# Cross-attention keys turned by VectorE in 32x32 blocks, scores on eight 32x64 tiles of TensorE, and each step's keys in two parts

## The reference

```python
scores = jnp.einsum('bsh,bqh->bsq', encoder_outputs, hidden)     # hidden = layernorm(x)
attn_weights = jax.nn.softmax(scores, axis=1)                    # over the keys s
context = jnp.einsum('bsq,bsh->bqh', attn_weights, encoder_outputs)
x = x + context
```

## Time and profile before

| | |
|---|---|
| median of three runs | 1027.85 us |
| profiled execution, span from first to last instruction | 1027.4 us |
| PE busy | 926.9 us, 90% |
| DVE busy | 484.5 us, 47% |
| ACT busy | 327.8 us, 32% |
| cross-attention, to the start of the next sublayer's projections (L544) | 320 us |
| one of its steps, from scores to scores | 37.4 us |

### The profile page before, as it was taken

How to read it: one execution, slowest core, us unless ns; L and a number is a source line. 1 busy time by engine, 2 the same in 40 slices (tenths; PEclk the granted TensorE clock), 3 DMA queues, 4 the chain that set the end, 5 groups by cost and what they waited for, 6 DMA issues and landing times.

```text
span 1027.4 us, 14956 instructions
## 1 busy us (share of the span) xinstructions
PE 926.9 (90%) x5233; PEld 678.6 (66%) x5249; DVE 484.5 (47%) x1124; ACT 327.8 (32%) x860; POOL 342.7 (33%) x170
## 2 busy tenths in 40 slices
PE   5999999999989997799897999979998999998960
PEld 5645645655646866788775667657876888886840
DVE  5723523433445025444467676786355333333404
ACT  3303412421433212655215565652330221111210
POOL 0000000000033233436101523454376999991015
PEclk9999999999999798899999999989999999998985
DMA  9642651561442003001109000003048344451117
GB/s 347 263 188 76 250 226 67 218 255 68 188 174 82 1 1 124 1 1 38 31 13 377 1 1 0 1 1 123 2 153 292 106 158 165 169 184 41 51 50 225
DMA packets 41257, 121.00 MB, mean 118 GB/s; under 512 B 3696, under 2 KB 7792, under 8 KB 37120
## 3 DMA queue, kind: packets, MB, share of 16 engines
q1 hardware_dynamic: 32320, 100.52, 26.0%
q10 hardware_dynamic: 6336, 11.54, 3.3%
q0 software_dynamic: 2560, 8.39, 2.5%
HBM read 102.05 MB, written 18.38 MB: 117 GB/s over the span
## 4 chain that ended last, share of the span: by engine, by line
PE 75%; POOL 7%; DVE 5%; DMA 5%; issue 4%; ACT 3%; SPq 0%; POOLq 0%; ACTq 0%; DVEq 0%
PE bank L499 9%; PE bank L457 8%; PE bank L477 7%; PE bank L955 5%; PE bank L957 5%; PE bank L956 5%; PE bank L771 2%; DMA nat<-in_ctx_keys 2%; PE bank L728 2%; PE bank L657 2%; PE bank L544 2%; POOL x_slots L1163 2%; PE bank L784 2%; PE bank L546 1%; PE bank L545 1%
## 5 line engine op out<-in xcount | busy, mean ns | idle before, releaser
L1193 ACT COPY ctxT<-bank 128x512 f32<-128x512 f32 (+1 forms) x104 | 60.1, 578 | 188.5 <-PE bank L457 187.7
L457 PE MATMUL bank<-cst,nat 128*128 128x128 f32 (+1 forms) x832 | 101.9, 278 | 10.4 <-DMA nat<-in_ctx_keys 9.8
L1049 POOL TENSOR_TENSOR wq_lo<-wq_raw,wq_hi 128x1024 fp32r<-128x1024 f32 x4 | 9.3, 2360 | 296.8 <-ACT wq_hi L1241 296.8
L457 PEld LDWEIGHTS bank<-cst,nat 128*128 128x128 f32 (+1 forms) x832 | 89.3, 143 | 22.3 <-issue 8.3
L499 PE MATMUL bank<-nat,probT 128*64 128x512 f32 (+1 forms) x416 | 91.0, 594 | 3.9 <-ACT probT L1199 3.9
L477 PE MATMUL bank<-ctxT,qT 128*64 128x400 f32 (+1 forms) x512 | 87.5, 499 | 0.8 <-DVE qT L1549 0.8
L1193 DVE COPY ctxT<-bank 128x512 f32<-128x512 f32 (+1 forms) x104 | 69.8, 671 | 31.1 <-PE bank L457 30.3
L1177 POOL TENSOR_TENSOR ring_lo<-ring_raw,ring_hi 128x2048 fp32r<-128x2048 f32 x18 | 82.9, 4604 | 1.4
L1103 POOL TENSOR_TENSOR sp<-sp,s_inv 128x512 f32<-128x512 f32 x32 | 32.6, 1040 | 139.9 <-DVE s_inv L1861 139.9
L955 PE MATMUL bank<-ring_hi,xg_lo 128*128 x176 | 73.4, 417 | 0.4 <-DVE y L2074 0.4
L477 PEld LDWEIGHTS bank<-ctxT,qT 128*64 128x64 f32 x512 | 37.2, 136 | 50.8 <-issue 49.8
(11 more groups left out here) (273 smaller groups left out, 2054.4 us busy)
## 6 DMA issues: line engine op xcount, KB each, us to landing
nat<-in_ctx_keys SPq DMA_DIRECT2D x32, 1536.0 KB, 12.7
ring_raw<-in_Wexp SPq DMA_DIRECT2D x21, 1024.0 KB, 9.2
x_slots<-zeros SPq DMA_DIRECT2D x1, 5632.0 KB, 25.7
hn<-x_slots ACTq DMA_DIRECT2D x22, 256.0 KB, 3.0
y_slots<-hn ACTq DMA_DIRECT2D x22, 256.0 KB, 2.1
w_raw<-in_Wexp SPq DMA_DIRECT2D x3, 1024.0 KB, 10.0
nat<-in_ctx_keys SPq DMA_DIRECT2D x16, 130.0 KB
wq_raw<-in_Wq SPq DMA_DIRECT2D x1, 2048.0 KB, 8.0
```

What stands on the lines that cost most here:

```text
L457: last = nc.tensor.transpose(bank[4 + g % RING][:, c * P:c * P + n], nat[par][0:n, b, j, c * P:(c + 1) * P], ident[0:n, 0:n])
L1193: copy(ctxT[b][:, :, j * P:j * P + n], src).then_inc(sem_done, 1)
```

## The change

Seven edits that belong together.

1. TensorE's key transposes, their ring of banks and the copies out of them go. VectorE turns the keys itself with its 32x32 block transpose, straight from `nat` to `ctxT` (`columns`): every 32x32 block is turned in place, so feature block j (of 16) of the keys in partition strip i (of 4) lies in strip i. `ctxT` is now [128, 2, 16, 416]: feature within the block in the partition, 13 x 32 keys a strip.
2. The scores contract over 32 features at a time. A matmul takes strip i, batch b and feature block j: 32 rows by 64 columns of the array, and the keys of strip i go to PSUM bank i (`scores4`, one tensor over banks 0 to 3). Sixteen feature blocks accumulate. A step has 2 parts x 16 x 2 x 4 = 256 such matmuls where it had 32.
3. The queries must stand in the same 32-row strips, four times: query_transposes is 64 matmuls with 32 output columns against the identity, into banks 4 to 7, copied to `q4` (in `hn`'s space) by ScalarE (three) and VectorE (one).
4. A step's keys are turned and scored in two parts, blocks 0 to 6 and 7 to 12 (`PARTS`); VectorE's four pairs of transposes for the next step are put between its other work.
5. The keys are loaded in three pieces as the context product releases them (`PIECES`, `context_part`), and the first step's in four (`FIRST`).
6. Because the probabilities stand in the order of the blocks, the exponentials read `scores4` across banks: three of 512 elements, one of 64, one of 1. Their transposes and the context product go in four groups (f), each released by its own exponential and copy.
7. GpSimd clears the rows of the last block that no key fills (`tails_cleared`); SP waits for that before the first keys.

Thirteen copies have become eight block transposes, two ahead of the maxima and two behind the step's last statistics. The diff, cut to its core:

```diff
-S_CHUNKS = [(0, 401), (401, 400), (801, 400), (1201, 400)]
-RING = 3
-T_FILLS = 2 * JT
+B32 = 32
+NB = D // B32
+KEYS_IN = [JT * B32, JT * B32, JM * B32 + TAIL - 2 * B32, JM * B32]
 P_FILLS = -(-JT // 4)
-BLOCK = T_FILLS + P_FILLS
-assert BLOCK % RING == 0 and BLOCK % 2 == 0
+PROB_BANK = [4, 5, 6, 4]
+EXPS = JM // 4 + 2
+TA = 7
+PARTS = [(0, TA), (TA, JT)]
+FIRST = [(0, 3), (3, TA), (TA, 10), (10, JT)]
+PIECES = [(0, TA), (TA, JM), (JM, JT)]
...
+            scores4 = whole.enter_context(nc.psum_tensor("scores4", [P, 4, 512], F32))
...
+        hn4 = sbuf(ctx, "hn", [P, 4, D])
+        hn = [hn4[:, i, :] for i in range(4)]
+        q4 = hn4[:].rearrange("p a (b q) -> p (a b) q", q=P)
...
-        ctxT = [sbuf(scope, f"ctxT{i}", [P, HC, SK]) for i in range(2)]
-        prob = sbuf(scope, "prob", [P, SK])
+        ctxT = sbuf(scope, "ctxT", [P, 2, NB, JT * B32])
+        prob = sbuf(scope, "prob", [P, JT, P])
...
+            sp.wait_ge(tails_cleared, 2)
+            load_first()
...
-                    sp.wait_ge(context_full, 2 * i + par + 1)
-                    load_keys(2 * i + par + 2, par)
-            sp.wait_ge(context_full, NT - 1)
+                    for p, (j0, j1) in enumerate(PIECES):
+                        sp.wait_ge(context_part, 3 * (2 * i + par) + p + 1)
+                        load_piece(2 * i + par + 2, par, j0, j1)
+            sp.wait_ge(context_part, 3 * (NT - 1))
...
@@ TensorE: the key transposes go, the query transposes and the scores change
-            def key_transposes(k, par, blk, g0):
-                turn = 16 * (k // 2 + 1) if isinstance(k, int) else k
-                for b in range(2):
-                    for j in range(JT):
-                        for p, (j0, _) in enumerate(PIECES):
-                            if j == j0:
-                                pe.wait_ge(keys_loaded[par][b][p], turn)
-                        g = g0 + b * JT + j
-                        n = P if j < JM else TAIL
-                        ring_free(blk, g)
-                        for c in range(HC):
-                            last = nc.tensor.transpose(bank[4 + g % RING][:, c * P:c * P + n],
-                                                       nat[par][0:n, b, j, c * P:(c + 1) * P], ident[0:n, 0:n])
-                        last.then_inc(ring_full, 1)
...
+                for f in range(4):
+                    if f == 3 and not (isinstance(k, int) and k < 2):
+                        pe.wait_ge(y1_ready, k - 1)
+                    for j in range(4):
+                        at = (4 * f + j) * B32
+                        for i in range(4):
+                            last = nc.tensor.matmul(bank[4 + f][B32 * i:B32 * (i + 1), j * P:(j + 1) * P], qn[:, at:at + B32],
+                                                    ident, start=True, stop=True, skip_group_check=True)
+                    last.then_inc(qt_full, 1)
...
+            def scores(k):
+                pe.wait_ge(qt_act, 3 * k + 3)
+                pe.wait_ge(qt_dve, k + 1)
+                for h, (t0, t1) in enumerate(PARTS):
+                    pe.wait_ge(columns_ready, 8 * k + 4 * h + 4)
+                    for j in range(NB):
                         for b in range(2):
-                            last = nc.tensor.matmul(bank[n][64 * b:64 * b + 64, 0:w], qT[:, c, 64 * b:64 * b + 64],
-                                                    ctxT[b][:, c, s0:s0 + w], start=c == 0, stop=c == HC - 1,
-                                                    skip_group_check=True)
+                            for i in range(4):
+                                rows_i, at = slice(B32 * i, B32 * (i + 1)), slice(B32 * t0, min(B32 * t1, KEYS_IN[i]))
+                                last = nc.tensor.matmul(scores4[64 * b:64 * b + 64, i, at], q4[rows_i, j, 64 * b:64 * b + 64],
+                                                        ctxT[rows_i, b, j, at], start=j == 0, stop=j == NB - 1,
+                                                        skip_group_check=True)
...
@@ TensorE: a step
-                key_transposes(turn, 1 - par, k + 1, 0)
-                prob_transposes(k, k + 1, T_FILLS)
-                pe.wait_ge(qT_ready, k + 2)
-                context(k, par, k + 1, BLOCK - 1)
-                scores(k + 1, k + 1, T_FILLS - 1)
+                prob_transposes(k, 0)
+                prob_transposes(k, 1)
+                pe.wait_ge(qt_dve, k + 2)
+                context(k, par, 0)
+                prob_transposes(k, 2)
+                context(k, par, 1)
+                prob_transposes(k, 3)
+                context(k, par, 2)
+                context(k, par, 3)
...
@@ GpSimd
+            for t in nat:
+                nc.gpsimd.memset(t[2 * B32:P, :, JM, :], 0.0).then_inc(tails_cleared, 1)
...
@@ ScalarE: exps and a step
+            def exps(k):
+                act.wait_ge(nmax_ready, k + 1)
+                for n in range(JM // 4):
+                    nc.scalar.activation(prob[:, 4 * n:4 * n + 4, :].rearrange("p t (i e) -> p t i e", e=B32),
+                                         scores4[:, :, n * P:(n + 1) * P].rearrange("p i (t e) -> p t i e", e=B32), ACT.Exp,
+                                         bias=nmax[:, 0:1], accum_out=sums[:, n:n + 1]).then_inc(prob_ready, 1)
...
+                queries_out(k + 1)
+                exps(k)
+                probs_out(k)
...
@@ VectorE
+                dve.wait_ge(scores_full, 2 * k + 2)
+                chain.mark(dve.tensor_reduce(mx[:, 0:2], scores4[:, 0:2, 0:KEYS_IN[0]], AX, ALU.max))
+                for i in (2, 3):
+                    chain.mark(dve.tensor_reduce(mx[:, i:i + 1], scores4[:, i, 0:KEYS_IN[i]], AX, ALU.max))
...
+            def columns(par, b, j0, j1, t0, t1):
+                src = nat[par][:, b, t0:t1, B32 * j0:B32 * j1].rearrange("p t (j a) -> p t j a", a=B32)
+                dst = ctxT[:, b, j0:j1, B32 * t0:B32 * t1].rearrange("p j (t e) -> p t j e", e=B32)
+                dve.transpose(dst, src).then_inc(columns_ready, 1)
...
+            def step(k, par, turn):
                 queries(k + 1)
+                dve.wait_ge(scores_full, 2 * k + 1)
+                keys_columns(1 - par, turn, 0, 0)
                 maxima(k)
                 queries_out(k + 1)
-                for g in range(1, T_FILLS, 2):
-                    keys_out(k + 1, g, 0)
-                probs_out(k, k + 1, T_FILLS)
+                probs_out(k)
+                keys_columns(1 - par, turn, 0, 1)
+                denominators(k)
+                keys_columns(1 - par, turn, 1, 0)
                 finish(k)
+                keys_columns(1 - par, turn, 1, 1)
...
```

More of the change, by code:

```diff
@@ L482, in prob_transposes @@
[L482 to L485, removed]
-                    ring_free(blk, g)
-                    for j in range(4 * f, min(4 * f + 4, JT)):
-                        n = P if j < JM else TAIL
-                        last = nc.tensor.transpose(bank[4 + g % RING][0:n, (j % 4) * P:(j % 4 + 1) * P],
-                                                   prob[:, j * P:j * P + n], ident)
-                    last.then_inc(ring_full, 1)
@@ L493, in context @@
-            def context(k, par, blk, g_last):
-                for g in (g_last - 1, g_last):
-                    pe.wait_ge(evac_act if g % 2 == 0 else evac_dve, evacs(blk, g))
-                for j in range(JT):
+                for f in range(4):
[7 more added lines that the diff above has]
+                    last.then_inc(qt_full, 1)
@@ new lines, in prob_transposes @@
+            def prob_transposes(k, f, following=True):
+                pe.wait_ge(prob_ready, EXPS * k + (f + 1 if f < 3 else EXPS))
+                if f == 3:
+                    pe.wait_ge(probT_dve, k + 1)
+                elif following:
+                    pe.wait_ge(qt_act, 3 * k + 3 + f + 1)
+                for j in range(4 * f, min(4 * f + 4, JT)):
+                    n = P if j < JM else TAIL
+                    last = nc.tensor.transpose(bank[PROB_BANK[f]][0:n, (j % 4) * P:(j % 4 + 1) * P], prob[:, j, 0:n], ident)
+                last.then_inc(probT_full, 1)
@@ L497, in context @@
+            def context(k, par, f):
+                if f == 0:
+                    pe.wait_ge(probT_dve, k + 1)
+                else:
+                    pe.wait_ge(probT_act, 3 * k + f)
+                for j in range(4 * f, min(4 * f + 4, JT)):
                     n = P if j < JM else TAIL
@@ L547, in keys @@
                 last.then_inc(kT_full, 1)
-            pe.wait_ge(prob_ready, 4 * NT)
             for k in range(4):
                 norm_transposes(k)
-            context(NT - 1, 1, NT, P_FILLS - 1)
+            pe.wait_ge(y1_ready, NT - 1)
+            for f in range(P_FILLS):
+                context(NT - 1, 1, f)
             for k in range(4, 7):
@@ L1218, in step, with queries_out @@
[L1218 to L1230 removed]
+            def queries_out(k):
+                for f in range(3):
+                    act.wait_ge(qt_full, 4 * k + f + 1)
```

(36 more changed lines are left out.)

156 lines of the change are left out of this document (62 added, 94 removed).

## The result

The changed kernel takes 1046.66 us (median of 4 runs, 1043.73 to 1049.85) against 1030.01 us for the kernel before in the same runs: ratio 1.0162, 95% interval 1.0127 to 1.0196. It is slower by 1.6%, where 3% less time was forecast, and it lies just above the range. The profiled execution, the slowest of the four, took 1049.85 us with a span of 1047.8 us, 20.4 us more than the span before; the medians are 16.7 us apart.

A forecast was written before the change was run, and what follows sets the result against it. The prediction took TensorE to bound the kernel, PE busy 90% of the span. Its sum was 1027.4 - 2.6 (start) - 32.6 (six periods) + 3.1 (end) = 995.3, plus 0.45 from span to median: 996 us, range 972 to 1045.

The forecast's parts named there:

- The bound and what goes: Cross-attention loop: TensorE sets it, busy 219.97 of 224.70 us; the 104 key transposes, 12.7 us of each step, go.
- a TensorE that never waits for instructions: Loop period: scores of 13.8 us in one piece plus 18.2 make 32.0 us, gaps under 1 us, clock 1.00.
- The rate of the scores: Scores in each step: 512 records at 27 ns each, 13.8 us.
- the likely ends: Bounds set on a step's scores: 11.2 us with eight tiles at once, 14.5 us at 28.4 ns a record.
- Rival 3: Loop's head: instructions come late, each of two returns waits for a fetch, 6 to 25 us, 1002 to 1021; chance 0.12.
- The path after the scores: From the scores' last matmul through maxima, exponentials, probability transposes and context to the next scores: 18.2 us.
- rival 2: VectorE's block transposes run at half rate, 29.7 us a step, period 38.1, no gain: 1037 us; chance 0.10.
- Rival 1: Scores: narrow tiles do not run eight abreast, weights load one after another; period 41.3, 1061 us; chance 0.14.
- The start: Step 0: clears delay keys 1.2 us, nmax at 44.1, step 1's scores at 60.7 against 63.30: 2.6 us gained.
- six periods: Step 1's scores to step 7's: six periods, each 5.4 us shorter, 32.6 us less.
- last scores to the next sublayer's projections: End of the cross-attention: scores 2.9 us longer, path after them 0.2 more, 3.1 us lost.

## Why the prediction was wrong

**The bound and what goes: right.** TensorE sets the loop, and no key transpose is left.

**The failed step: a TensorE that never waits for instructions.** The forecast's period has the scores in one piece and "Gaps are under 1 us each, as now, so I keep the clock at 1.00". Both failed. From 104.03 to 122.6 the scores took 18.6 us for the 13.8 forecast: 12.1 at full rate, 4.6 in pauses and 1.7 by the slower clock in the portion after the first pause. From step 1's scores to step 7's the pauses marked issue come to 37.8 us, 6.3 a period, and the mean granted clock is 0.93.

**The rate of the scores: near.** The forecast took 27 ns a record, near the 28.4 of a burst of 32 in the earlier trace rows, and multiplied by 512: 13.8 us a step. The array did better, 3.19 us for 128 records of 224 keys and 2.85 for 128 of 160 to 192, so 12.1 us a step, between the likely ends; the assumption that tiles of different rows run at once held. The Trainium skill, TensorE: Matmul & The Clock Gate, section on the gap of 56 ns, is not borne out for these tiles in its floor of about 25 ns: the 128 starts of the portion at 117.90 are 19.9 ns apart in the mean.

**Rival 3 had the mechanism and was mis-sized.** It priced a fetch at each of two returns to the loop's head, 6 to 25 us in all. The fetches came in every step: 28 pauses, 50.1 us. What was at hand and not used: the loop's records go from 948 to 2820, the DMA engines are busy for 0.44 of the loop, and 128 records at 23 ns last 3 us, no longer than the small transfer of 3.0 us in the earlier trace rows takes. Blocks that come 3.1 to 4.2 us apart on idle DMA engines, and 5.7 to 6.4 beside keys, cannot keep up with that.

**The path after the scores: right.** 18.2 us forecast; from 122.6 to the context's end at 141.2 it was 18.6. VectorE's block transposes took 1752 ns for 1536 elements and 2021 ns for 1792, 15.1 us a step for 14.9 (14.8 by the forecast's own rows), and the scores waited for them in step 0 alone; this settles rival 2:

```profile
L1559 DVE STREAM_TRANSPOSE ctxT<-nat x64: 1734/1779/2272, 15.0 to 305.3; 128x1536 f32<-128x1536 f32 x34, 128x1792 f32<-128x1792 f32 x28, 128x2048 f32<-128x2048 f32 x2
```

**Rival 1: wrong.** It needed 36 ns a matmul; unpaused ones take 22 to 25.

**The start.** The clears delayed the first key DMA by 0.95 us (2.61 against 1.66), near the 1.2 taken. But the forecast had step 0 set by VectorE, with nmax done at 44.1, and the first scores hidden; these were themselves late. The changed kernel's start, with the first maxima:

```profile
22.96 7.52 PE L474 MATMUL scores<-ctxT,hn 32*64 32x224 f32 x222 [8.63 <-DVE ctxT L1559]
32.72 4.60 PE L474 MATMUL scores<-ctxT,hn 32*64 32x224 f32 x128 [2.24 <-issue]
38.91 2.85 PE L474 MATMUL scores<-ctxT,hn 32*64 32x160 f32 x128 [1.60 <-issue]
45.11 1.86 PE L474 MATMUL scores<-ctxT,hn 32*64 32x160 f32 x34 [3.34 <-issue]
```

```profile
47.01 1.02 DVE L1550 TENSOR_REDUCE mx<-scores 128x2 f32<-128x832 f32 x1 [5.31 <-PE scores L474]
```

They end at 47.0 with 7.2 us of pauses, the maxima wait 5.31 us for TensorE, nmax is done at 49.2, and step 1's scores start at 67.04, not 60.7.

**The sum by terms**, forecast and measured on the spans:

| | forecast | measured |
|---|---|---|
| to step 1's scores (63.30 before) | -2.6 | +3.7 |
| six periods | -32.6 | +10.3 |
| last scores to the next sublayer's projections | +3.1 | +7.6 |
| the rest | 0 | -1.2 |
| sum | -32.1 | +20.4 |

43 of the 52 us missed lie in the six periods, 7.2 us in each. The run without key loads shows how they divide: its six periods from step 1 on are 33.2 us in the mean, so 6.0 of the 39.2 come of the keys' traffic. Its trace against the changed kernel's divides the 6.0: pauses marked issue of 12.5 us for 37.8, which is 4.2 a period, and a TensorE busy for 181.8 us at a granted clock of 0.99 for 192.3 at 0.93, which is 1.8. The 33.2 lie only 1.2 over the forecast's 32.0 because 2.1 of short pauses stand against scores that were forecast 1.7 too long. At the end the last step's scores took 19.0 us for 10.9 before (2.9 more was forecast), again by pauses and clock; the path after them was 0.5 us shorter.

## What to carry to other kernels

Cutting matmuls into small tiles multiplies instructions, and a load and a matmul every 23 ns use up a block of 256 in 3 us: count the instructions of a dense stretch, and of a loop's body, before the columns. The cure here was the same arithmetic in half as many instructions, the two parts cut along the contraction instead of along the keys, and a loop body small enough to be held; that turned 1.6% slower into 5% faster. In a profile the sign is idle marked issue between portions of exactly 128 matmul records, worst where the DMA engines are full. Whether a loop is held shows in the instruction queue: no packet in the loop's later iterations.

## What the hardware showed that was not expected

- The body of a TensorE loop was held at 1348 load and matmul records (29 packets fetched in the whole run) and at 948, and was fetched again at 1796 (51 packets), with 34 register, branch and semaphore instructions beside the 1348 and the 1796. Held, the looped form fetches fewer packets than the one written out (29 for 40, 26 for 34); not held, it fetches more (51 for 47, 67 for 63). The Trainium skill, Runtime: NRT & Kernel Launch, section on instruction fetch, gives room for 2048; here less could be used.
- While TensorE used them up faster, blocks of instructions came 3.1 to 4.2 us apart with idle DMA engines and 5.7 to 6.4 us apart beside keys at about 400 GB/s.
- A pause of a few us in a dense stretch can cost twice: the portion of 128 records behind the 2.41 us pause at 109.20 ran at a granted clock of 0.64 and took 4.69 us for 3.01. It does not each time: behind an equal pause at 189.77 the same portion had 1.00, and the clock fell to a mean of 0.72 only after the next, of 3.01 us.
- fp32 matmuls on 32x64 tiles, eight at a time, sustained 22 to 25 ns a record with 160 to 224 keys and 45 ns with 416; on 128x64 tiles of 50 keys, two at a time, 31 ns.
